# Four query and key projections per sequence, spread over partitions by DMA through DRAM, in place of sixteen onto padded head stacks

## The reference

```python
# layer 0, attention: 16 heads of 8 channels, on the normalised x
y = softmax(mask(heads(x@Wq+bq) @ heads(x@Wk+bk).T / sqrt(8))) @ heads(x@Wv+bv)        # self, causal
y = y + softmax(heads(x@Wcq+bcq) @ heads(ctx@Wck+bck).T / sqrt(8)) @ heads(ctx@Wcv+bcv)  # cross
x = x + y @ Wp + bp
# layer 0, ffn: 8 experts 128 -> 512 -> 128 with relu, the two best of the router's weights
# layer 1, attention: one head of 128 channels, queries from x, keys and values from ctx
# layer 1, ffn: 16 heads of 64 channels; each head's value is a mixture of 2 of 8 value experts,
#               its output is given to 2 of 8 output experts
```

## Time and profile before

| | before |
|---|---|
| median of 3 runs | 1322.04 us (1322.01 to 1323.66) |
| the profiled execution | 1322.67 us; its span from first to last instruction 1320.9 us |
| mean granted TensorE clock | 0.847 |
| PE / PEld busy | 86% / 67% of the span |
| DVE / ACT / POOL busy | 53% / 37% / 6% |
| DMA | 56.85 MB, mean 43 GB/s |

### The profile page before, as it was taken

One profiled execution on the slowest core, in us unless ns is written; L12 is line 12 of the kernel. 1 busy time (PEld: TensorE's weight loads), 2 busy tenths in 40 slices (PEclk: granted clock), 3 DMA queues, 4 the chain that ended last, 5 costly groups with the idle time before them and its releaser, 6 DMA issues.

```text
span 1320.9 us, 21222 instructions
## 1 busy us (share of the span) xinstructions
PE 1137.6 (86%) x8499; PEld 883.2 (67%) x8499; DVE 706.6 (53%) x1867; ACT 494.1 (37%) x1022; POOL 85.0 (6%) x134
## 2 busy tenths in 40 slices
PE   6888779989989988989988988988998998985696
PEld 4547545777668765877577855976577766874475
DVE  5514466646565557547665658546664656423500
ACT  4233415352534425451634334442535253422120
POOL 0010002000110002000200011000200011000000
PEclk8558959899789979998889978998889978977556
DMA  7000000242020420142022221042023210133222
GB/s 212 0 1 4 3 0 1 48 69 65 8 49 17 69 55 21 29 76 57 6 49 47 47 47 46 5 77 63 1 48 67 64 40 13 29 56 84 52 44 52
DMA packets 198032, 56.85 MB, mean 43 GB/s; under 512 B 173568, under 2 KB 193838, under 8 KB 197934
## 3 DMA queue, kind: packets, MB, share of 16 engines
q1 hardware_dynamic: 195630, 51.20, 19.9%
q10 hardware_dynamic: 2304, 4.29, 1.1%
HBM read 31.36 MB, written 24.12 MB: 42 GB/s over the span
## 4 chain that ended last, share of the span: by engine, by line
PE 75%; DVE 11%; ACT 7%; issue 3%; SPq 3%; DMA 2%; ACTq 0%; DVEq 0%
PE bank L928 10%; PE bank L737 10%; PE bank L773 9%; PE bank L884 5%; PE bank L663 5%; PE bank L843 4%; PE bank L624 3%; PE bank L678 3%; PE bank L588 3%; DVE negmax L1261 3%; ACT pa L1022 3%; PE bank L942 2%; PE bank L860 2%; PE bank L688 2%; PE bank L911 2%
## 5 line engine op out<-in xcount | busy, mean ns | idle before, releaser
L1022 ACT ACTIVATE pa<-bank 128x512 f32<-128x512 f32 x224 | 123.4, 596 | 122.8 <-PE bank L678 75.8
L1261 DVE TENSOR_REDUCE negmax<-bank 128x2 f32<-128x512 f32 (+1 forms) x224 | 139.0, 683 | 41.9 <-PE bank L526 22.1
L1039 ACT ACTIVATE pa<-bank,b_c 128x256 f32<-128x256 f32 x256 | 107.5, 471 | 128.6 <-PE bank L737 127.3
L928 PE MATMUL bank<-vb,pb 128*128 128x65 f32 x1024 | 137.1, 299 | 4.2 <-issue 4.2
L928 PEld LDWEIGHTS bank<-vb,pb 128*128 128x128 f32 x1024 | 132.8, 214 | 10.3 <-issue 7.9
L737 PE MATMUL bank<-xnT_a,w 128*128 128x256 f32 x512 | 138.1, 417 | 0.1
L773 PE MATMUL bank<-w,pa 128*128 128x128 f32 x1024 | 124.2, 276 | 0.0
L773 PEld LDWEIGHTS bank<-w,pa 128*128 128x128 f32 x1024 | 121.9, 192 | 3.2
L1101 ACT ACTIVATE pb<-bank 128x512 f32<-128x512 f32 x128 | 69.9, 602 | 125.4 <-PE bank L888 125.4
L737 PEld LDWEIGHTS bank<-xnT_a,w 128*128 128x128 f32 x512 | 101.1, 208 | 17.3 <-ACT pa L1039 0.5
L1415 DVE TENSOR_REDUCE negc<-bank 128x2 f32<-128x512 f32 x128 | 80.0, 684 | 58.8 <-PE bank L860 58.6
(11 more groups left out here) (240 smaller groups left out, 1706.3 us busy)
## 6 DMA issues: line engine op xcount, KB each, us to landing
v_d<-at SPq DMA_DIRECT2D x32, 256.0 KB, 3.3
vb<-v_d SPq DMA_DIRECT2D x32, 256.0 KB, 6.0
at_d<-at SPq DMA_DIRECT2D x32, 256.0 KB, 2.1
at<-at_d SPq DMA_DIRECT2D x32, 256.0 KB, 4.4
pv_d<-pvs SPq DMA_DIRECT2D x8, 512.0 KB, 3.1
pvs<-pv_d SPq DMA_DIRECT2D x16, 256.0 KB, 4.2
w<-in_L_ffn_W_dram ACTq DMA_DIRECT2D x1, 2048.0 KB, 11.5
bd<-mix_d SPq DMA_DIRECT2D x128, 8.0 KB
```

Of the source, the lines that this page charges most:

```text
L928: mm = pe.matmul(BB[2 + qt][:, i * (DH + 1):(i + 1) * (DH + 1)], pb[:, h % NPB, kt * T + qt * P:kt * T + (qt + 1) * P], vb[:, kt, h, :], s ...
L1022: nc.scalar.activation(pa[:, e % NPA, :], BA[e % 2][:, :], ACT.Exp, scale=SC0).then_inc(S["a_ex"], 1)
L1039: ins = nc.scalar.activation(hT[:, u % 4, c, :], BA[u % 2][:, c * T:(c + 1) * T], ACT.Relu, bias=b1_c[:, k:k + 1])
L1261: nc.vector.tensor_reduce(negmax[:, i:i + ng], BA[j][:, :].rearrange("p (g k) -> p g k", g=ng), AX, ALU.max, negate=True).then_inc(S["a_mx ...
```

## The change

1. **Projection.** `w_heads` holds one 128 x 128 matrix for each kind, its columns in the order (channel, head). `f_heads(half)` multiplies two of them (half 0 cross, half 1 self): 4 projections in place of 16. ACT writes the four `hi` parts, DVE the four `lo` parts.
2. **Spreading.** SP writes each `hi` part twice and each `lo` part once to the DRAM tensors `q_d` and `k_d` (8 DMAs, 256 KB and 128 KB), and `f_spread(half)` reads them back into the strips of `qs` and `ks`: 16 DMAs of 25 or 24 partitions x 4 head groups x 1 KB. The row of ones is written into `q_d` or stands in `ks` from the start.
3. **Time.** These steps come earlier: `f_norm_apply` behind `a_project`, `f_heads` ahead of `a_router`, `f_spread` 0 behind `a_expert` 3 and `f_spread` 1 behind `c_out`. `xn_f` and a double `cxT` are tiles of their own for that, and x_f + bias goes to `x_a`, so that `x_f` is free earlier.
4. **The order tables** of both streams are new.
5. **POOL** clears `bd` in eight memsets of 256 columns, each time in place of one of 2048.
6. **Start.** No zeroed weight stack; two DVE instructions blank `qs` and `ks`; the loads of layer 1's weights (`last_loads`) are issued behind the first spreading, and the transposes of these weights (`s_turn`) start behind `a_max` 3 instead of `a_max` 0.

```diff
-        w_stack = sb("w_stack", [P, 4, G, P])
+        w_heads = sb("w_heads", [P, 4, P])
+        lo_part = sb("lo_part", [P, 4, T], F32R)
+        q_d = dram("q_d", [ROWS, H, 2, T])
+        k_d = dram("k_d", [ROWS, H, 2, T])
-        KINDS = (Q0, K0, QC, KC)
+        KINDS = (QC, KC, Q0, K0)
-                   ("f_load", 0), *run("a_score", 2, 14), ("a_lastpv", 0), ("a_heads", 0), ("a_project", 0),
-                   ("c_kv", 0), ("a_norm2", 0), ("a_norm2_apply", 0), ("a_router", 0), *run("a_expert", 0, 3),
-                   ("f_norm", 0), *run("a_expert", 3, 8), ("f_norm_apply", 0), ("a_last", 0), ("c_norm", 0),
-                   *run("f_stack", 0, 4), ("c_norm_apply", 0), ("c_q", 0), ("f_stack", 4), ("c_max", 0),
-                   ("f_stack", 5), ("f_stack", 6), ("c_turn", 0), ("c_out", 0), ("f_stack", 7)]
+                   ("a_project", 0), ("f_norm_apply", 0), ("a_norm2", 0), ("c_kv", 0), ("a_norm2_apply", 0),
+                   ("f_heads", 0), ("f_heads", 1), ("a_router", 0), *run("a_expert", 0, 4), ("f_spread", 0),
+                   *run("a_expert", 4, 8), ("a_last", 0), ("c_norm", 0), ("c_norm_apply", 0), ("c_q", 0),
+                   ("c_max", 0), ("c_turn", 0), ("c_out", 0), ("f_spread", 1)]
...
# SP
-                            sp.wait_ge(S["a_x1"], upto("a_x1", 0))
+                            sp.wait_ge(S["a_xb"], upto("a_xb", 0))
+                    def f_heads(half):
+                        for u in (2 * half, 2 * half + 1):
+                            rows_d, kind = (k_d if u % 2 else q_d)[:, :, SELF if half else CROSS], KINDS[u]
+                            first = 0 if u % 2 else D
+                            sp.wait_ge(S["a_mh"], upto("a_mh", u + 1))
+                            sp.dma_start(rows_d[first:first + 2 * D].rearrange("(r d) h n -> (d h) r n", d=D),
+                                         hi_part[:, kind, :].unsqueeze(1).broadcast_to([P, 2, T])).then_inc(S[f"f_hw{half}"], 16)
+                            rest = 2 * D - 2 * first
+                            sp.wait_ge(S["a_split"], upto("a_split", u + 1))
+                            sp.dma_start(rows_d[rest:rest + D].rearrange("d h n -> (d h) n"), lo_part[:, kind, :].bitcast(F32))\
+                                .then_inc(S[f"f_lw{half}"], 16)
+                    def f_spread(half):
...
+                        for j in range(4):
+                            for stack, rows_d, n in ((qs_all, q_d, ROWS), (ks_all, k_d, ROWS - 1)):
+                                sp.dma_start(stack[32 * j:32 * j + n, :, sc, :].bitcast(F32),
+                                             rows_d[0:n].rearrange("r (g j) s n -> j s r g n", j=4)[j, sc])\
+                                    .then_inc(S[f"f_st{half}"], 16)
...
# PE
-                    def f_stack(u):
-                        for c in range(2):
-                            g = 2 * (u % 2) + c
-                            rows, rhs = (CC, cxT_a) if kind == KC else (P, xnT_f)
-                            mm = pe.matmul(BA[2 + u % 2][:, c * T:(c + 1) * T], w_stack[0:rows, kind, g, :], rhs[:, :],
-                                           start=True, stop=True)
+                    def f_heads(half):
+                        if half == 0:
+                            pe.wait_ge(S["f_xc"], upto("f_xc", 1))
+                        if now[0] > 0 and half == 1:
+                            pe.wait_ge(S["a_x1"], upto("a_x1", 0))
+                        for c in range(2):
+                            kind = KINDS[2 * half + c]
+                            rows, rhs = (CC, cxT[now[0] % 2]) if kind == KC else (P, xnT_f)
+                            mm = pe.matmul(BA[half][:, c * T:(c + 1) * T], w_heads[0:rows, kind, :], rhs[:, :],
+                                           start=True, stop=True)
+                        mm.then_inc(S["a_pj"], 1)
# PE, a_max
-                            pe.wait_ge(S["a_split"], upto("a_split", 16))
+                            pe.wait_ge(S["f_st0"], upto("f_st0", 128))
+                        if m == 4:
+                            pe.wait_ge(S["f_st1"], upto("f_st1", 128))
# PE, hidden
+                        elif now[0] + 1 < B:
+                            pe.wait_ge(S["a_split"], upto("a_split", 4 + 2 * u + 2))
# ACT
+                    def f_heads(half):
+                        act.wait_ge(S["a_pj"], upto("a_pj", half + 1))
+                        for u in (2 * half, 2 * half + 1):
+                            kind = KINDS[u]
+                            nc.scalar.activation(hi_part[:, kind, :].bitcast(F32R), BA[half][:, (u % 2) * T:(u % 2 + 1) * T],
+                                                 ACT.Identity, bias=bias_c[:, kind:kind + 1]).then_inc(S["a_mh"], 1)
# DVE
+                            nc.vector.scalar_tensor_tensor(lo_part[:, kind, :], BA[half][:, (u % 2) * T:(u % 2 + 1) * T],
+                                                           bias_c[:, kind:kind + 1], hi_part[:, kind, :],
+                                                           ALU.add, ALU.subtract).then_inc(S["a_split"], 1)
# POOL
+                    def clear_blocks():
+                        for i in range(8):
+                            nc.gpsimd.memset(bd[:, 256 * i:256 * i + 256], 0.0).then_inc(S["b_bz"], 1)
```

More of the change, by code:

```diff
@@ L360, in transformer_program @@
-        STEPS_B = [("b_norm", 0), ("b_norm_apply", 0), ("b_gates", 0), ("b_top2", 0),
-                   ("b_split", 0), ("b_split", 1), ("b_top2", 1), *run("b_split", 2, 5), ("b_top2", 2),
-                   *run("b_split", 5, 8), *run("b_max", 0, 8), ("b_shift", 0), ("b_score", 0), ("b_fill", 0),
-                   ("b_mix", 0), ("b_mix", 1), ("b_score", 1), ("b_sel", 0), ("b_score", 2), ("b_score", 3),
+        STEPS_A = [("a_values", 0), ("a_max", 0), ("f_load", 0), *run("a_max", 1, 7), ("a_shift", 0),
+                   ("a_score", 0), ("f_norm", 0), *run("a_score", 1, 14), ("a_lastpv", 0), ("a_heads", 0),
+                   ("a_project", 0), ("f_norm_apply", 0), ("a_norm2", 0), ("c_kv", 0), ("a_norm2_apply", 0),
+                   ("f_heads", 0), ("f_heads", 1), ("a_router", 0), *run("a_expert", 0, 4), ("f_spread", 0),
+                   *run("a_expert", 4, 8), ("a_last", 0), ("c_norm", 0), ("c_norm_apply", 0), ("c_q", 0),
+                   ("c_max", 0), ("c_turn", 0), ("c_out", 0), ("f_spread", 1)]
@@ new lines, in transformer_program @@
+        STEPS_B = [("b_norm", 0), ("b_norm_apply", 0), ("b_gates", 0), ("b_split", 0), ("b_top2", 0),
+                   ("b_split", 1), ("b_top2", 1), ("b_split", 2), ("b_split", 3), ("b_top2", 2),
+                   *run("b_split", 4, 7), ("b_fill", 0), ("b_split", 7), *run("b_max", 0, 8), ("b_shift", 0),
+                   ("b_mix", 0), ("b_score", 0), ("b_mix", 1), ("b_score", 1), ("b_sel", 0),
+                   ("b_score", 2), ("b_score", 3), ("b_attend", 0), ("b_score", 4), ("b_score", 5),
+                   ("b_attend", 1), ("b_score", 6), ("b_score", 7), ("b_attend", 2), ("b_attend", 3),
+                   ("b_gather", 0), ("b_weigh", 0), ("b_gather", 1), ("b_out", 0)]
@@ new lines, in transformer_program @@
+        AFTER_A = (51, 62, 65, 66, 68, 69, 72, 72, 73, 73, 74, 76, 76, 76, 78, 86, 87, 88, 88, 91, 91, 92, 92, 93,
+                   94, 95, 95, 95, 97, 100, 101, 104, 105, 106, 107, 107, 108, 108, 109, 112, 112, 112, 113)
+        assert len(AFTER_A) == len(STEPS_B)
+        LAST_B = [("b_norm", 0), ("b_norm_apply", 0), ("b_gates", 0), ("b_top2", 0),
+                   ("b_split", 0), ("b_split", 1), ("b_top2", 1), ("b_split", 2), ("b_top2", 2),
+                   *run("b_split", 3, 8), *run("b_max", 0, 4), ("b_fill", 0), ("b_sel", 0),
+                   ("b_mix", 0), ("b_mix", 1), *run("b_max", 4, 8), ("b_shift", 0), *run("b_score", 0, 4),
@@ L407, in merged @@
                     order.append((name, i, q))
-                if q == 0 and (name, i) in once_after:
-                    order.append(once_after[(name, i)] + (0,))
+                if q == 0:
+                    order += [("s_turn", n, 0) for n in turns.get((name, i), ())]
             return order
@@ L958, in _ @@
                     own = dict(s_first=s_first, s_cols=s_cols, s_rows=s_rows, s_bias=s_bias, s_turn=s_turn,
-                               f_norm_apply=f_norm_apply, f_stack=f_stack, a_values=a_values, a_max=a_max, a_shift=a_shift,
+                               f_norm_apply=f_norm_apply, f_heads=f_heads, a_values=a_values, a_max=a_max, a_shift=a_shift,
                                a_score=a_score, a_lastpv=a_lastpv, a_heads=a_heads, a_project=a_project, a_norm2_apply=a_norm2_apply,
@@ L987, in s_cols @@
                         act.wait_ge(s_const, N_CONST)
[L988 removed]
+                        act.wait_ge(s_colc, 3)
                     def s_turn(n):
@@ L1114, in _ @@
                     own = dict(s_first=s_first, s_cols=s_cols, s_turn=s_turn,
```

(2 more changed lines are left out.)

205 lines of the change are left out of this document (82 added, 123 removed).

## The result

The changed kernel takes 1368.57 us (median of four runs, 1353.57 to 1396.08), the kernel before 1322.03 beside it: a ratio of 1.0275, interval 1.0229 to 1.0321. The ratio leaves out runs that the comparison counts as disturbed; the medians alone give 1.035. By the medians it is 47 us slower, by the ratio 36, where I forecast 36 us faster. Its runs are spread over 3%, those of before over 0.4%; the profiled one took 1362.30 (span 1360.6).

A forecast was written before the change was run, and what follows sets the result against it. TensorE was taken to set the pace, with DMA having room. Six steady sequences -28, first sequence -4.5, last -3, start -1 and tail +1 sum to -35.5 us: 1286.5 from a median of 1322.04, range 1264 to 1312.

The forecast's parts named there:

- The clock: TensorE's clock in the new handover: busy some 11 of 14.6 us, could lose up to 2 us; +1.0 us taken per steady sequence.
- rival 1: TensorE, less dense, halves speed: 3 us more after `a_project`, 1 more in the handover; total about 1310 us, chance 0.16.
- In both places PE's row is as full as now: Argument against half speed after `a_project` and in the handover: TensorE as busy there as before; no size of its own.
- This is no forecast: in the handover they filled PE: Dropped projections free 55.5 us of TensorE busy time, not counted as gain because they filled it during a serial chain.
- The handover, -8.0: From one sequence's experts to the next `a_values`: 22.6 us without moved steps before, 14.6 after, so -8.0 per steady sequence.
- Behind `a_project`, +2.3: From `a_project`'s end to the third hidden matmul group: 9.7 us without a moved pair, about 12.0 after, so +2.3.
- The sequence, -4.7: One steady sequence: -8.0 handover, +2.3 after `a_project`, +1.0 clock, so -4.7 us; six of them -28.
- The round trip in the steady sequences: Writes to and reads from DRAM on SP's queue, ahead of `a_max` 4: cost nothing, slack 10 us.
- rival 3: SP's queue is the bound: reads issue too slowly, `a_max` 4 waits; at 3.2 us an issue about 1349, chance 0.09.
- The start, -1 with bounds of -4 and +10: First, uncovered round trip against the wait for transposed weights, moved three maxima on: net -1 us, bounds -4 and +10.
- The quick trip: First DRAM write and read under 6 us, by about 2.0 us plus bytes per DMA; start gains 7, unused in sum.
- The end, -3 and +1: Last sequence -3 us, losing a 4.00 us wait but gaining chain waits; tail +1 from SP's order, bounds -3 and +5.

## Why the prediction was wrong

**The step that failed is "The clock".** It read "could lose up to 2; I take +1.0", and rival 1 put 3 us and 1 us more on the two stretches. Both priced the half clock over the stretch that is thin. The trace after shows the price behind it: the clock went down at 446, when the handover was over, and stayed for 50 us of attends and scores; 45.2 us for two falls, 22.6 each. The direction was rival 1's, but a fall cost 22.6 us where I had 1.0 and rival 1 had 2.0 in the handover. "In both places PE's row is as full as now" was the sentence behind the small price, and the record says otherwise: PE is busy in 26.65 of the 29.99 us of the handover in rows 4, and in 10.54 of 13.57 here, with four waits and none of the sixteen wide projections.

**What is shown of the cause, and what isn't.** Filling the handover removed the falls (1324.8), filling the experts didn't (1386.0), and they came without the round trip too (1376.8). Counted over the profiled runs of the changed kernel and its variants: of 48 steady handovers with spare matmuls in or right behind them none was followed by attends at half clock, of 24 without them 7 were. But these 24 include the six of the kernel with added matmuls amid the attends, of which none fell. And handovers alike in every record fell and didn't within one run. A thin handover makes a fall possible; what decides it, and what the new order adds, stays open.

**"This is no forecast: in the handover they filled PE".** Right, and not taken far enough: sixteen projections stood in the handover (12 went, 4 moved out of it), and wide matmuls there also hold the clock. Eight unread ones in their place do, and four do.

**The handover, -8.0: right within 1 us.** From the last product's end to `a_values` I had 14.6 us; in order of time it is 443.57 - 430.0 = 13.6 (13.6 to 14.7 in all six), and the memset in eight pieces leaves `xn_a` 0.68 us (2.05 in rows 4):

```profile
427.96 2.05 PE L805 MATMUL bank<-w,pa 128*128 128x128 f32 x16
...
432.97 2.24 POOL L1172 MEMSET bd<- 128x256 f32 x8 [55.87 <-PE bank L943]
...
433.28 0.68 DVE L297 TENSOR_SCALAR xn_a<-x_a,mv_a,rstd_a 128x128 f32<-128x128 f32 x2
...
435.31 0.70 PE L826 MATMUL bank<-xnT_a,wq 128*128 128x256 f32 x2 [0.86 <-ACT xnT_a L1080]
...
443.57 0.71 PE L626 MATMUL bank<-wv,xnT_f 128*128 128x128 f32 x4 [0.77 <-DVE x_mid L1392]
```

The port rule of the Trainium skill ("SBUF — State Buffer", Who interferes with whom) agrees: pieces let the vector engine in.

**Behind `a_project`, +2.3: near, by luck.** 10.6 us before, 10.3 in the mean of six sequences; in the sequence shown 706.42 - 693.2 = 13.2, and 13.3 in the mean (12.2 to 13.7): +3.0. But the terms that I added up there (0.7, 2.1, 0.6 and 1.1) make 4.5, not 2.3, and the projections did not run at the full clock: from 697.91 to 702.12 they take 4.2 us in place of 2.1, at a granted clock of 0.50, as rival 1 had it. So the terms on ACT and DVE were mostly covered.

```profile
692.47 0.71 PE L753 MATMUL bank<-wp,yT 128*128 128x128 f32 x4 [0.46 <-ACT yT L1050]
...
706.42 1.99 PE L769 MATMUL bank<-xnT_a,w 128*128 128x256 f32 x8
```

**The sequence, -4.7:** without a fall 141.8 against 145.4, the mean of before's last five periods: -3.6. The missing microsecond lies ahead of `a_project`: the stretch from `a_values` to its end grew by 6.8 us (74.8 to 81.6 in the mean of the same sequences) where the steps moved into it were priced at 4.9. Which of them takes the rest stays open.

**The round trip in the steady sequences: nothing, right.** PE's only wait on `qs` or `ks` from DMA is the first; SP's queue had its slack, and rival 3 (slower by SP) gave the right sign by the wrong cause.

**The start, -1 with bounds of -4 and +10: off within its bounds.** The first maximum's matmuls are done at 33.9, not near 30, and the wait for the transposed weights was not covered but grew from 3.22 us to 5.16, because SP now issues those loads behind the 16 reads:

```profile
15.50 0.50 SPq L458 DMA_DIRECT2D k_d<-lo_part  x1
...
23.91 0.88 SPq L471 DMA_DIRECT2D qs<-q_d  x1
...
33.06 0.80 PE L654 MATMUL bank<-ks,qs 32*128 32x256 f32 x8 [11.49 <-DMA ks<-k_d]
...
48.69 1.11 PE L594 MATMUL bank<-ident,pb 128*128 128x128 f32 x4 [5.16 <-DMA pb<-in_L_ffn_Wo_dram]
...
60.60 1.76 PE L670 MATMUL bank<-ident,negmax 128*128 128x128 f32 x7 [1.59 <-DVE negmax L1271]
```

`a_shift` starts 6.6 us later than before (53.97), and the first sequence behind it gained 2.1 us where I had 4.5. The last write that the first read waits for was issued at 15.5 and landed at 23.8: 8.3 us, where 2.4 to 2.5 is the median of such writes, and 2.2 in the kernel of 1286.0 us, which loads the expert weights later. The quick trip of the Trainium skill ("DMA: Bandwidth & Descriptors", Anatomy of one DMA), which the page gives for DMAs issued by GpSimd while these are SP's, doesn't hold while the engines carry the expert weights. In the run that issues those loads behind `s_turn(0)`, PE's wait is halved.

**The end, -3 and +1:** +13.4. 7.2 of it come ahead of the last handover's attends: `a_values` comes early because steps were moved behind it, and at the end they have to be done (a steady sequence has +6.8 in that half and gets it back in its handover). The rest is attends at half clock, 4.88, 7.09 and 13.91 where before had 7.06, 3.79 and 7.36. The wait of 4.00 us did shrink, to 1.42.

## What to carry to other kernels

Before taking wide matmuls out of a stretch where TensorE waits on a chain, look at the granted clock there and behind it, and price a fall over all that follows until the clock comes back, not over the thin stretch. A few unread wide matmuls in the waits cost next to nothing and gave 44 us here by the medians, and another 34 at the end of the kernel, where the clock had never been held throughout. Compare two versions with the clock held in both: only so was the change's own worth (2 to 3 us a sequence) to be seen. A kernel whose runs lie 3% apart is itself a sign that its clock falls in some of them.
